# Edge scores of a graph attention layer: sources split by 112, two digits of the upper number as rows of the one-hot operand, a mask in the table, one maximum out of PSUM

## The reference, cut to what matters

```python
xp = (layernorm(x) @ W).reshape(3125, 4, 256)          # 4 heads
a_src = einsum("nhc,hc->nh", xp, att_src)              # one number per node and head
a_dst = einsum("nhc,hc->nh", xp, att_dst)
e = leaky_relu(a_src[src] + a_dst[dst], 0.2)           # per edge and head
m = segment_max(e, dst); ee = exp(e - m[dst]); ...     # softmax over the edges of a node
x = x + relu(segment_sum(xp[src] * alpha, dst) + bias)
x = x + moe_ffn(layernorm(x))
```

## Time and profile before

| | us |
|---|---|
| Time, median of 3 runs (lowest, highest) | 2160.78 (2157.02, 2161.48) |
| Span of the profiled execution, first to last instruction | 2296.1 |
| First block, on PE | 0 to 320.2 |
| Second block, first matmul to DVE's last sum | 332.7 to 482.7 |
| Everything behind it | 482.7 to 2296.1 |

### The profile page before, as it was taken

The page is one execution under the profiler, slowest core; times in us unless marked ns, Lnnn a source line. Parts: engine busy times, 40 slices in busy tenths (PEclk is TensorE's granted clock), DMA queues, the critical chain, the costliest instruction groups (busy, mean ns, idle before and its releaser), DMA issues. The chain is left out here.

```text
span 2296.1 us, 53233 instructions
## 1 busy us (share of the span) xinstructions
PE 1959.2 (85%) x14846; PEld 1318.7 (57%) x14847; DVE 1470.6 (64%) x4341; ACT 1137.3 (50%) x2499; POOL 768.2 (33%) x943
## 2 busy tenths in 40 slices
PE   6999977667878888888888589983899999999997
PEld 4666545645766667777667455652454445555553
DVE  7988859987666666666666699867543443443333
ACT  4444421113666666676666566654543443443332
POOL 1020000022555555555555232321233333333332
PEclk9999976568999999999999889995899999999999
DMA  7444544403988888888888677746646556644542
GB/s 272 134 143 136 172 131 172 186 0 114 312 281 291 286 299 287 294 296 287 287 298 294 235 249 240 228 142 234 233 169 249 212 167 239 221 160 171 176 162 80
DMA packets 135664, 490.15 MB, mean 213 GB/s; under 512 B 16900, under 2 KB 17108, under 8 KB 133410
## 3 DMA queue, kind: packets, MB, share of 16 engines
q0 software_dynamic: 95568, 334.62, 43.5%
q1 hardware_dynamic: 31954, 125.15, 15.1%
q10 hardware_dynamic: 8064, 29.36, 3.7%
HBM read 419.17 MB, written 81.17 MB: 218 GB/s over the span
## 5 line engine op out<-in xcount | busy, mean ns | idle before, releaser
L1130 PE MATMUL main_ps<-rows,O 128*128 128x256 f16 x4992 | 619.2, 283 | 125.7 <-DVE acc L1066 66.3
L1113 ACT ACTIVATE O<-O,pk 128x128 f16<-128x128 f16 x1664 | 502.9, 387 | 246.1 <-DVE O L1083 203.5
L1130 PEld LDWEIGHTS main_ps<-rows,O 128*128 128x128 f16 x4992 | 480.9, 102 | 217.9 <-issue 72.8
L1052 POOL DMA_INDIRECT rows<-projected,idx x416 | 395.5, 951 | 325.2 <-PE small_ps L1135 202.9
L1087 DVE TENSOR_SCALAR O<-O,pk 128x128 f16<-128x128 f16 x1664 | 314.6, 273 | 15.0 <-issue 0.2
L1837 PE MATMUL x_h<-w_p,gram 128*128 x1344 | 307.1, 386 | 18.4 <-ACT gram L1787 7.6
L1852 PE MATMUL x_o<-w_p,gram 128*128 x1344 | 308.0, 379 | 1.4 <-ACT gram L1806 1.4
L1886 PE MATMUL pj_ps<-gram,xsT 128*125 128x512 f16 x1200 | 271.1, 385 | 8.8 <-ACT xsT L402 5.5
L1837 PEld LDWEIGHTS x_h<-w_p,gram 128*128 128x128 f16 x1344 | 131.6, 99 | 171.6 <-issue 31.5
L1886 PEld LDWEIGHTS pj_ps<-gram,xsT 128*125 128x125 f16 x1200 | 163.2, 139 | 104.7 <-ACT xsT L402 8.6
L1083 DVE TENSOR_SCALAR O<-iota,pk 128x128 f16<-128x128 f16 x416 | 109.4, 263 | 164.9 <-PE small_ps L1135 124.1
(11 more groups left out here) (346 smaller groups left out, 2538.9 us busy)
## 6 DMA issues: line engine op xcount, KB each, us to landing
w_f<-in_L_ffn_W_dram SPq DMA_DIRECT2D x14, 2048.0 KB
b_t<-in_L_ffn_b_dram ACTq DMA_DIRECT2D x56, 512.0 KB
projected_f<-xp_f POOLq DMA_DIRECT2D x25, 500.0 KB, 3.7
projected<-xp POOLq DMA_DIRECT2D x25, 500.0 KB, 4.6
out_dram<-n_x SPq DMA_DIRECT2D x25, 500.0 KB
x_after_gnn_normed<-PK POOLq DMA_DIRECT2D x25, 500.0 KB, 9.1
xt<-in_x_dram SPq DMA_DIRECT2D x24, 512.0 KB, 3.3
n_own<-projected_f SPq DMA_DIRECT2D x24, 512.0 KB, 13.0
```

Of the source, the lines that this page charges most:

```text
L1052: pool.indirect_dma_start(out=rows[:, 4 * p + k, :, :].rearrange("k n d -> k (n d)"), out_offset=None, in_=xp_d[:, :], in_offset=bass.Indi ...
L1113: ins = act.activation(O[:, k, 1 + HEADS + h, :], O[:, k, 0, :], ACT.Copy, scale=pk[:, p, k, w:w + 1])
L1130: pe.matmul(main_ps[:, h * C:(h + 1) * C], O[:, k, 1 + HEADS * a + h, :], rows[:, 4 * p + k, b, h * C:(h + 1) * C], start=first and h % 2 ...
```

## The change

A source is split as s = 112 * hi + lo, so that `lo` needs only 112 of the 128 partitions and `hi` runs over 28 numbers. `hi` is split again into two digits, hi = 7 * tens + ones. The operand that was the one-hot `lo` now has three parts: rows 0 to 111 compare with `lo`, rows 112 to 119 with the first digit, rows 120 to 127 with the second. The table gets 16 more rows, which hold -65504 wherever a column's digit differs from the row's. So the product is the source's term at the edge's own `hi` and that minus 65504 or more everywhere else, and one maximum over `hi` straight out of PSUM replaces the multiply and the sum. The digits are stored to DRAM in the first block, and each load of a chunk is now three DMAs: `lo` to 112 partitions, the two digit rows to 8 partitions each, `dloc` to 128. The table `terms` (128 rows, 2 parts, 28 x 4 columns) is put together at the end of the first block: PE writes the mask into PSUM, adds the nodes' terms from their 125-row blocks by 52 matmuls with a shifted identity (two or three for each block), and DVE copies it out once. `hi_oh`, its eight builds, the turning of `hi`, `pick` and `total` are gone. PE's wait on `s_sel` becomes one on `s_got` (the maximum of group n - 2).

```diff
-HI = -(-NODES // P)
+LOW, TENS, DIGITS = 112, 7, 8
+HI = -(-NODES // LOW)
+MASK = -65504.0
...
+        def load_numbers(sp, lo, dl, vs, done):
+            sp.dma_start(lo[0:LOW], lo_d[vs, :].partition_broadcast(LOW)).then_inc(done, 16)
+            sp.dma_start(lo[LOW:P], digits_d[:, vs, :].rearrange("n v k -> n (v k)").unsqueeze(1).broadcast_to([2, DIGITS, CHUNK * P])).then_inc(done, 16)
+            sp.dma_start(dl, dloc_d[vs, :].partition_broadcast(P)).then_inc(done, 16)
...
+                            sp.dma_start(digits_d[0].rearrange("(p r) n -> p (r n)", r=4), rowV[:, 2, :]).then_inc(s_vstore, 16)
+                            sp.dma_start(digits_d[1].rearrange("(p r) n -> p (r n)", r=4), rowV[:, 3, :]).then_inc(s_vstore, 16)
-                    sp.wait_ge(s_vstore, 32)
-                    sp.wait_ge(s_tr_ix, 3)
-                    for t, d in ((stage_lo, lo_d), (stage_dl, dloc_d)):
-                        sp.dma_start(t, d[0:CHUNK, :].partition_broadcast(P)).then_inc(s_row[0], 16)
+                    sp.wait_ge(s_vstore, 64)
+                    sp.wait_ge(s_tr_ix, 2)
+                    load_numbers(sp, stage_lo, stage_dl, slice(0, CHUNK), s_row[0])
...
                         link(dve.tensor_scalar(fV[:, 1, :], fV[:, 1, :], -WHOLE, None, ALU.add))
-                        dve.scalar_tensor_tensor(fV[:, 2, :], fV[:, 1, :], -float(ROWS), fV[:, 0, :], ALU.mult, ALU.add)
+                        dve.scalar_tensor_tensor(rowV[:, 0, :], fV[:, 1, :], -float(LOW), fV[:, 0, :], ALU.mult, ALU.add)
+                        link(dve.tensor_scalar(fV[:, 2, :], fV[:, 1, :], 1.0 / TENS, -0.5 * (TENS - 1) / TENS, ALU.mult, ALU.add))
+                        link(dve.tensor_scalar(fV[:, 2, :], fV[:, 2, :], WHOLE, None, ALU.add))
+                        link(dve.tensor_scalar(fV[:, 2, :], fV[:, 2, :], -WHOLE, None, ALU.add))
+                        dve.tensor_copy(rowV[:, 2, :], fV[:, 2, :])
+                        dve.scalar_tensor_tensor(rowV[:, 3, :], fV[:, 2, :], -float(TENS), fV[:, 1, :], ALU.mult, ALU.add)
...
-                        dve.tensor_copy(rowV, fV[:, 2:4, :]).then_inc(s_rowv, 1)
+                        dve.tensor_copy(rowV[:, 1, :], fV[:, 3, :]).then_inc(s_rowv, 1)
...
-                        t = (srcT, hiT, dlocT)[n]
+                        t = (srcT, dlocT)[n]
...
-                    def high_one_hots(n):
-                        if n == 0:
-                            dve.wait_ge(s_trc, 2)
-                        vs = slice(n * CHUNK, (n + 1) * CHUNK)
-                        dve.tensor_tensor(hi_oh[:, vs, :], iota16[:, 0:HI].unsqueeze(1).broadcast_to([P, CHUNK, HI]),
-                                          hiT[:, vs].unsqueeze(2).broadcast_to([P, CHUNK, HI]), ALU.is_equal).then_inc(s_hioh, 1)
+                    def digit_mask():
...
-                        dve.tensor_scalar(stage_lo, stage_lo, iota_col[:, 0:1], None, ALU.is_equal)
+                        dve.tensor_scalar(stage_lo, stage_lo, src_row[:, 0:1], None, ALU.is_equal)
...
-                        if i in (15, 17, 19):
+                        if i in (15, 17):
                             turned_numbers((i - 15) // 2)
+                        if i == 16:
+                            digit_mask()
                         if 14 <= i < 14 + KD:
                             low_wp(i - 14)
-                        if 17 <= i < 25:
-                            high_one_hots(i - 17)
...
+                    dve.wait_ge(s_spread, 1)
+                    dve.tensor_copy(terms[:, :, :, :], spread_ps)
...
-                        if i in (13, 15, 17):
+                        if i in (13, 15):
                             turn_numbers((i - 13) // 2)
+                    pe.wait_ge(s_trc, 2)
+                    pe.matmul(spread_ps, ident16[:, :], mask[:, :, :, :], start=True, stop=True, skip_group_check=True)
+                    for n, blocks in enumerate((range(LATE), range(LATE, BLOCKS))):
+                        pe.wait_ge(s_st16, 2 * n + 2)
+                        for b in blocks:
+                            for a in range(ROWS * b // LOW, (ROWS * (b + 1) - 1) // LOW + 1):
+                                w = P - (ROWS * b - LOW * a)
+                                ins = pe.matmul(spread_ps[0:LOW, :, a, :], shift16[0:ROWS, w:w + LOW],
+                                                st16[:, b, :].rearrange("r (n g h) -> r n g h", n=2, g=2)[:, :, 0, :],
+                                                start=False, stop=True, skip_group_check=True)
+                    ins.then_inc(s_spread, 1)
...
-                        for t, d in ((lo_b, lo_d), (dl_b, dloc_d)):
-                            sp.dma_start(t[p], d[CHUNK * i:CHUNK * (i + 1), :].partition_broadcast(P)).then_inc(s_row[p], 16)
+                        load_numbers(sp, lo_b[p], dl_b[p], slice(CHUNK * i, CHUNK * (i + 1)), s_row[p])
...
-                        dve.wait_ge(s_row[p], 32 * (j + 1))
-                        dve.tensor_scalar(lo_b[p], lo_b[p], iota_col[:, 0:1], None, ALU.is_equal)
+                        dve.wait_ge(s_row[p], 48 * (j + 1))
+                        dve.tensor_scalar(lo_b[p], lo_b[p], src_row[:, 0:1], None, ALU.is_equal)
...
-                            if not early(n, 2):
-                                dve.wait_ge(s_got, n - 1)
                             dve.wait_ge(s_grp, n + 1)
-                            dve.tensor_tensor(pick[:, b, :, :, :], s_ps[b][:, :, :].rearrange("k v (a h) -> k v h a", h=HEADS),
-                                              hi_oh[:, four(n), :].unsqueeze(2).broadcast_to([P, 4, HEADS, HI]), ALU.mult).then_inc(s_sel, 1)
-                            if not early(n, 1):
-                                total(n - 1, 1 - b)
+                            four = slice(4 * n, 4 * n + 4) if isinstance(n, int) else bass.ds(4 * n, 4)
+                            dve.tensor_reduce(sT[:, four, :], s_ps[b][:, :, :].rearrange("k v (a h) -> k v h a", h=HEADS), AX.X, ALU.max).then_inc(s_got, 1)
...
-                                pe.wait_ge(s_sel, n - 1)
+                                pe.wait_ge(s_got, n - 1)
...
-                                    pe.matmul(s_ps[(p + q) % 2][:, u, :].rearrange("k (a h) -> k a h", h=HEADS), lo_b[p][0:ROWS, 4 * q + u, :],
-                                              st16[:, :, h0:h0 + HEADS], start=(part == 0), stop=(part == 1))
+                                    pe.matmul(s_ps[(p + q) % 2][:, u, :], lo_b[p][:, 4 * q + u, :],
+                                              terms[:, part, :, :].rearrange("r a h -> r (a h)"), start=(part == 0), stop=(part == 1))
```

More of the change, by code:

```diff
@@ L254, in program @@
             fV = cut(VP, 8 * ROW4, 4 * ROW4, None).rearrange("v (n a) -> v n a", n=4)
-            rowV = cut(VP, 12 * ROW4, ROW4, F16).rearrange("v (n a) -> v n a", n=2)
+            rowV = cut(VP, 6 * ROW4, 2 * ROW4, F16).rearrange("v (n a) -> v n a", n=4)
+            shift16 = sbuf(c, "shift16", [P, 3 * P], F16)
+            digit = sbuf(c, "digit", [P, 4])
+            digits_of = sbuf(c, "digits_of", [P, 3, HI])
+            mask = sbuf(c, "mask", [P, 2, HI, HEADS], F16)
+            s_spread = sem("ed_spread")
             cnt = sbuf(c, "cnt", [98, BLOCKS - 1])
@@ L591, in term_parts @@
                         dve.tensor_tensor(st16[:, bs, 2 * HEADS:], stN[:, bs, :], st16[:, bs, 0:2 * HEADS], ALU.subtract).then_inc(s_st16, 1)
-                    def high_one_hots(n):
-                        if n == 0:
-                            dve.wait_ge(s_trc, 2)
-                        vs = slice(n * CHUNK, (n + 1) * CHUNK)
-                        dve.tensor_tensor(hi_oh[:, vs, :], iota16[:, 0:HI].unsqueeze(1).broadcast_to([P, CHUNK, HI]),
-                                          hiT[:, vs].unsqueeze(2).broadcast_to([P, CHUNK, HI]), ALU.is_equal).then_inc(s_hioh, 1)
+                    def digit_mask():
+                        dve.memset(shift16[:, 0:P], 0.0)
+                        dve.memset(shift16[:, 2 * P:], 0.0)
+                        dve.tensor_copy(shift16[:, P:2 * P], ident)
+                        link(dve.tensor_scalar(digit[:, 0:1], iota_col[:, :], LOW - 0.5, -float(LOW), ALU.is_gt, ALU.mult))
+                        link(dve.tensor_scalar(digit[:, 1:2], iota_col[:, :], LOW + DIGITS - 0.5, -float(DIGITS), ALU.is_gt, ALU.mult))
+                        link(dve.tensor_tensor(digit[:, 2:3], digit[:, 0:1], digit[:, 1:2], ALU.add))
+                        link(dve.tensor_tensor(src_row[:, :], iota_col[:, :], digit[:, 2:3], ALU.add))
+                        link(dve.tensor_scalar(digits_of[:, 0, :], iota_row[:, 0:HI], 1.0 / TENS, -0.5 * (TENS - 1) / TENS, ALU.mult, ALU.add))
+                        link(dve.tensor_scalar(digits_of[:, 0, :], digits_of[:, 0, :], WHOLE, None, ALU.add))
+                        link(dve.tensor_scalar(digits_of[:, 0, :], digits_of[:, 0, :], -WHOLE, None, ALU.add))
```

(9 more changed lines are left out.)

25 lines of the change are left out of this document (9 added, 16 removed).

## The result

The changed kernel takes 2204.6 us (2203.0 to 2209.0) against 2158.9 for the kernel before on the same chip: 1.021 times its time, 95% interval 1.0194 to 1.0226, 45.7 us slower. The direction was forecast; the size was not: 19.6 us of loss were forecast (2180) and 45.7 measured, and 2204.6 lies above the range of 2154 to 2192.

A forecast was written before the change was run, and what follows sets the result against it. DVE looked like the bound, with the chain from load issue to next issue a second bound as long. Second block +17.3 and late projection +2.3 gave +19.6 on 2160.8: 2180.4 us, range 2154 to 2192.

The forecast's parts named there:

- The reading of a group: Second block: 104 maxima at 0.62 us replace 104 `pick` and 104 sums; DVE's 1.08 us a group becomes 0.62.
- The floor of 1.04: Second block: PE needs 1.04 us a group, with a register load of 0.33 us that no faster DVE removes.
- The landing is the second bound, just met, and DVE's small wait hides it: Second block: the chain issue, landing, build, last four groups, issue bounds as long as DVE, 17.94 us a cycle.
- The digits go over two engines: Chunk's load: a source with leading count 2 puts 8 whole rows on each of two engines, 23 rows for 16.
- The load's 3.7 us: Chunk's load: seven more rows at 0.53 us move the landing from 11.3 to 15.0 us behind the issue.
- theory P2: From the experiments: rows slow down where two engines write one of 16 groups of 8 partitions at the same time.
- The sum: Whole kernel: +17.3 us in the second block and +2.3 in the late projection, +19.6 together.
- rival 1: Chunk's load: the digits use 16 engines, landing 11.6 us behind the issue, cycle 18.0, total 2157 us; chance 0.12.
- The upper bound: Second block: with 4.8 us a load in place of 3.7, six builds give +6.6, so 24 us of loss.
- The late projection: Its load takes 3.7 us longer but is issued 1.4 us earlier: +2.3 us.
- The end of the first block: PE's 53 small matmuls, at most 3.5 us, and DVE's 0.4 us copy lie beside POOL's last store: cost nothing.
- Rival 3: Chunk's load: the digits go over one engine, 31 rows, 8.0 us a load, total 2211 us; chance 0.03.

The follow-up runs named there:

- a_old_load: Changed kernel with the load of before: lo to all 128 partitions in one transfer, digits' transfer left out (scores not right): 2154.2 us, ratio 0.9967.
- a_2h: Changed kernel, each load's three transfers cut by visits into halves of 28 and 24, asked for sooner: 2161.3 us, ratio 1.0004 to the kernel before.
- b_cut16: Kernel before with its lo transfer cut into 112 and 16 leading rows: 2177.8 us, ratio 1.0088.
- a_last: Changed kernel with the digits' transfer issued last of the three, behind that of dst_local: 2182.8 us, 1.0088 of the kernel before.
- a_16: Changed kernel with each digit stored eight times in DRAM, so the digits' transfer reads 16 rows: 2178.1 us, ratio 1.0066 to the kernel before.
- b_8c: Kernel before with the number row brought in eight transfers of 16 rows, each to 16 neighbouring partitions: 2232.3 us, ratio 1.0316.
- b_8s: Kernel before with the number row brought in eight transfers of 16 rows, each to partitions at steps of 8: 2181.1 us, ratio 1.0088.
- a_one: Changed kernel with number row (14 times) and both digits in one 16-row DRAM table, loaded in one transfer: 2191.1 us, 1.0139 of the kernel before.
- b_p120: Kernel before, number row as 120 rows to partitions 0 to 119, then [2, 4] rows to 120 to 127 over two engines: 2205.2 us, 1.0197.
- b_p0: Kernel before, number row as 120 rows to partitions 8 to 127, then [2, 4] rows to 0 to 7 over two engines: 2194.0 us, 1.0147.

## Why the prediction was right and wrong

- *The reading of a group*: right. 104 maxima at 0.623 us (0.62 foreseen), groups 1.02 to 1.09 apart (1.04), the eight matmuls 0.92 for 0.84 (+0.08). The floor of 1.04 was priced at the 1.2 GHz level alone; it holds at 2.4 GHz too (a_old_load).
- *The landing is the second bound, just met, and DVE's small wait hides it*: right. It is what turned a gain of 7 us into a loss of 46, and a_2h, which asks for the same bytes sooner, takes the whole loss away.
- *The digits go over two engines*: right. The tail is there (share 0.12, 50 GB/s, from about 401.2 to 405.5 us), and b_cut16 has none. Its 4.3 us fit 8 rows at 0.53; 3.7 were taken, for seven rows.
- *The load's 3.7 us, "because the other engines are in full use beside it as in the first row"*: **the step that failed**. I took a row's 0.53 us from whole transfers and carried it to rows that go elsewhere. A build was to begin 15.0 us behind the issue and began 19.0 behind it. The 213 GB/s with all engines busy show the missing 4.0: rows of 0.7 to 1.0 us ahead of the tail. Two causes were found. The 112 rows at seven an engine meet in some groups of partitions (0.71 to 0.75 us a row, a_last and b_cut16; that they meet is theory P2, not seen row by row), and the two engines at the digits slow `dst_local` down to 0.99 (0.51 when the digits come last). The second is the size of the miss: 8 rows x 0.48 = 3.8 us. a_last, which has the tail but not this, costs 19.3 us with builds some 15.2 behind the issue, close to the 19.6 and 15.0 of the forecast. That this is so close is partly luck, since its 112 rows are slow too, 1.3 us a load that the forecast didn't have.
- *The sum*: right in form. With 19.0 for 15.0 at six builds it gives 17.3 + 6 x 4.0 = 41.3 for the second block; 42.0 were measured. The gain without the load was put too low: rival 1 had 2.5 us in the block and 3.6 in all, a_old_load 6.5 and 7.4, with cycles of 17.7 us as a mean for the 18.0 of rival 1. The upper bound failed with the term: I had looked for the slowest row in a store of 125 rows (4.8 us), which has 5 engines and writes DRAM. Nothing in the trace of before shows several engines in one group of partitions, and I should have said that the price of a new shape has no upper row.
- *The late projection*: +2.3 foreseen, +4.9 at the turning of block 23. The load was issued at 266.73, 2.1 us sooner than before (1.4 foreseen), and its build came 21.7 us behind (14.6 before): the same failed term, 7.0 for 3.7.
- *The end of the first block*: right. 46 small matmuls take 2.52 us and six more 0.47, with the one of the mask 53 as counted, beside POOL; the next block starts 6.6 us behind the end of POOL's last issue (328.98 + 0.52 to 336.09), as before.
- *The rivals*: rival 1 (all 16 engines) is what a_16 tests: 2178, not 2157, since it counted only the tail. Rival 3's 2211 is near the result by luck: its 15 more rows on one engine are not what the trace shows, a tail on two.

## What to carry to other kernels

A load that lands just before it is needed is a bound, whatever the wait beside it says; a transfer that is cut anew must be priced by its slowest engine and by where its rows go, not by bytes. Keep transfers over all 128 partitions whole; if one must be cut, put the small piece last in the queue (26 us here), and issue the load earlier by halves (44 us here) before trying to make it fast. A price taken from rows of another shape is a lower end, and when no row shows the shape, the range should be open above.

## What the runs showed of the hardware

- With all 16 engines busy, the rate was 411 GB/s or 118 in one load of b_8c. Rows of 13,312 bytes took 0.51 us in whole transfers, and in pieces of 16 rows 1.03 at steps of 8 partitions (b_8s) and 1.79 in 16 neighbours (b_8c), by the destination alone. A cut into two halves of 64 doubled the row's time (1.02).
- A DMA share of 1.00 says only that each engine is at work on a row, not how fast: 417 and 214 GB/s in one load of a_one.
- Two engines at a small transfer slowed a whole one beside it to half its rate when they wrote partitions 112 to 127 (213 for 417 GB/s, kernel after and a_last) or 120 to 127 (207, b_p120), and hardly when they wrote 0 to 7 (374, b_p0).
- A group of PE's took 1.04 us at a granted clock of 0.50 and of 1.00 (kernel after, a_old_load).
